# Attention and experts on one core: ScalarE copies the attention output out of PSUM, GpSimd divides it

## The reference

```python
x = x + xattn(layernorm(x), ctx)      # 16 heads of 32, 2048 keys
x = x + ffn(layernorm(x))             # 32 experts, the best 4 of a token, and a shared one
# in xattn, for each head:
q, k = fq_sym(q * scale), fq_sym(k)   # rounded to 8 bits per row
v = fq_sym(v, axis=keys)
attn = fq_unsigned(softmax(q @ k.T))  # rounded to 0..255 of the row's maximum
out = attn @ v
return concat(out) @ Wp + bp
```

## Time and profile before

| what | value |
|---|---|
| runs | 1444.52, 1453.22, 1441.58 us |
| median | 1444.52 us |
| profiled execution | 1447.9 us, of it a span of 1446.2 |
| mean granted TensorE clock | 0.978 |
| busy: TensorE / VectorE / ScalarE / GpSimd | 88 / 68 / 55 / 60 % of the span |

### The profile page before, as it was taken

One profiled execution on the slowest core, in us unless ns is written; L12 is line 12 of the kernel. 1 busy time (PEld: TensorE's weight loads), 2 busy tenths in 40 slices (PEclk: granted clock), 3 DMA queues, 4 the chain that ended last, 5 costly groups with the idle time before them and its releaser, 6 DMA issues.

```text
span 1446.2 us, 28685 instructions
## 1 busy us (share of the span) xinstructions
PE 1276.8 (88%) x7890; PEld 634.9 (44%) x7891; DVE 976.3 (68%) x1886; ACT 800.0 (55%) x1030; POOL 874.8 (60%) x894
## 2 busy tenths in 40 slices
PE   8999578888888888888887879999999999999995
PEld 3444134444444444444443434444444444444442
DVE  4567799999999999999999646823333333333332
ACT  2224499999999999999999742221222222222221
POOL 3223388899899999899888812243444444444443
PEclk9999799999999999999999889999999999999998
DMA  7565977786677667666677866465677777686442
GB/s 249 131 153 118 174 122 138 142 146 145 133 145 145 139 132 142 142 144 137 144 139 132 183 204 168 93 170 119 151 194 212 200 197 179 142 221 140 91 75 31
DMA packets 398568, 215.53 MB, mean 149 GB/s; under 512 B 356903, under 2 KB 357031, under 8 KB 398514
## 3 DMA queue, kind: packets, MB, share of 16 engines
q1 hardware_dynamic: 378338, 176.05, 51.7%
q0 software_dynamic: 20176, 38.83, 15.0%
HBM read 100.28 MB, written 37.49 MB: 95 GB/s over the span
## 4 chain that ended last, share of the span: by engine, by line
PE 36%; DVE 20%; issue 19%; DMA 13%; POOL 4%; ACT 4%; SPq 1%; DVEq 1%; POOLq 0%; ACTq 0%
PE psS L815 15%; DMA out_y<-mem 9%; DVE mem L579 7%; DVE mem L595 7%; PE psS L823 6%; PE psS L450 3%; POOL mem L669 3%; DMA mem<-mem 3%; ACT mem L536 2%; PE psS L1671 2%; PE psT L1280 1%; PE psP L807 1%; PE psAV L421 1%; DVE mem L1078 1%; PE psAV L1658 1%
## 5 line engine op out<-in xcount | busy, mean ns | idle before, releaser
L536 ACT ACTIVATE mem<-mem 128x2048 uint8<-128x2048 f32 x256 | 534.3, 2088 | 46.0 <-POOL mem L652 42.2
L669 POOL TENSOR_SCALAR mem<-mem 128x2048 bf16<-128x2048 uint8 x256 | 486.0, 1899 | 26.8 <-DMA mem<-mem 6.4
L450 PE MATMUL psS<-mem 128*128 128x512 bf16 x1024 | 313.2, 388 | 112.3 <-DVE mem L579 54.2
L815 PE MATMUL psS<-mem 128*128 (+1 forms) x752 | 348.6, 605 | 0.0
L595 DVE TENSOR_SCALAR_CACHE_REDUCE mem<-psS,mem 128x1024 f32<-128x1024 f32 x256 | 327.5, 1279 | 3.0 <-PE psS L450 2.9
L579 DVE TENSOR_SCALAR_CACHE_REDUCE mem<-psS 128x1024 f32<-128x1024 f32 x256 | 312.4, 1220 | 14.0 <-PE psS L450 11.8
L849 DVE TENSOR_SCALAR mem<-psS 128x512 f32<-128x512 f32 x94 | 64.9, 691 | 321.7 <-PE psS L815 312.5
L843 ACT ACTIVATE mem<-mem 128x256 f32<-128x256 f32 x94 | 39.1, 416 | 352.9 <-DVE mem L849 349.4
L1212 POOL DMA_INDIRECT out_y<-mem x78 | 124.3, 1593 | 170.4 <-DMA out_y<-mem 150.2
L815 PEld LDWEIGHTS psS<-mem 128*128 128x128 f32 x752 | 136.3, 191 | 146.7 <-issue 143.5
L823 PE MATMUL psS<-mem 128*128 (+1 forms) x376 | 179.0, 598 | 2.0 <-ACT mem L837 2.0
(11 more groups left out here) (210 smaller groups left out, 1177.1 us busy)
## 6 DMA issues: line engine op xcount, KB each, us to landing
mem<-in_moe_w SPq DMA_DIRECT2D x64, 768.0 KB, 5.7
mem<-xn_dram SPq DMA_DIRECT2D x32, 256.0 KB, 3.0
xn_dram<-mem SPq DMA_DIRECT2D x29, 256.0 KB, 2.2
mem<-in_x SPq DMA_DIRECT2D x28, 256.0 KB, 2.9
mem<-mem SPq DMA_TRANSPOSE x292, 3.1
mem<-in_ctx_in SPq DMA_DIRECT2D x16, 256.0 KB, 3.4
out_y<-mem SPq DMA_DIRECT2D x16, 256.0 KB, 2.2
mem<-in_wkv SPq DMA_DIRECT2D x2, 1024.0 KB, 7.8
```

What stands on the lines that cost most here:

```text
L450: last = nc.tensor.matmul(psS[c][:, k * D:(k + 1) * D], qT[pm][:, hm, :], kT[:, hm, c * HALF + k * D:c * HALF + (k + 1) * D], start=True, ...
L536: nc.scalar.activation(p8[slot], S[slot], ACT.Exp, bias=NB[:, slot:slot + 1], scale=sq[p][:, h:h + 1], accum_out=Z[p][:, h:h + 1]).then_in ...
L669: nc.gpsimd.tensor_scalar(pb[slot], pT[slot].bitcast(U8).rearrange("p (j q b) -> p j b q", b=2, q=P), 1.0, 0.0, ALU.mult, ALU.add).then_in ...
L815: last = nc.tensor.matmul(bankG[o], xT[o if xo is None else xo][:, c, :], w(c * 2 * I, 2 * I), start=(c == 0), stop=(c == DC - 1))
```

## The change

ScalarE copies the 128x512 outputs of a tile from `psAV` to a buffer in SBUF, `product_sb`, in step 7, ahead of that step's exponential. GpSimd multiplies this buffer by 1/Z into `an` at the end of its step 7, ahead of the scale of the queries (L628), and signals `attn_done`. VectorE keeps the reciprocal and loses the multiplication. The copy of the transposed output to `anT`, on ScalarE, moves from step 7 to step 8. TensorE's list isn't changed. `product_sb` lies in a part of SBUF that only the stage of the keys uses.

```diff
--- before.py
+++ after.py
@@ -136,6 +136,7 @@
         vT = cut(DC * TK).rearrange("p (c t) -> p c t", c=DC)
         vT8 = cut(DC * TK // 4, I8).rearrange("p (c t) -> p c t", c=DC)
         ks = [cut(D) for _ in range(2)]
+        product_at = at[0] - 2 * D
         behind_keys = at[0]
         k8 = cut(D // 4, I8)
         kr = cut(D)
@@ -153,6 +154,7 @@
         anT = cut(D).rearrange("p (c t) -> p c t", c=DC)
         x1 = cut(D)
         xn2 = cut(D)
+        product_sb = mem[:, product_at:product_at + D]
         at[0] = behind_keys
         p8 = [cut(TK // 4, U8) for _ in range(NS)]
         pT = [cut(TK // 4, U16) for _ in range(NS)]
@@ -226,6 +228,7 @@
 
 
         attn_done = sem("attn_done")
+        product_out = sem("product_out")
         attn_ev = sem("attn_ev")
         attn_mm = sem("attn_mm")
         attn_tr = sem("attn_tr")
@@ -514,7 +517,13 @@
             if h == 0 and there(t + 1):
                 act.wait_ge(query_tr, t + 2)
                 nc.scalar.activation(xnT.rearrange("p c t -> p (c t)"), psT[:], ACT.Copy).then_inc(query_ev, 1)
-            if h == 7 and there(t - 1):
+            if h == LAG and there(t - 1):
+                if due(H * t):
+                    act.wait_ge(av_done, H * t)
+                if due(t - 1):
+                    act.wait_ge(attn_done, t - 1)
+                nc.scalar.activation(product_sb, psAV[1 - p][:], ACT.Copy).then_inc(product_out, 1)
+            if h == 8 and there(t - 1):
                 if due(t):
                     act.wait_ge(attn_tr, t)
                 if due(t - 1):
@@ -581,12 +590,9 @@
             if h == LAG and there(t - 1):
                 if due(H * t):
                     dve.wait_ge(av_done, H * t)
+                if due(t - 1):
+                    dve.wait_ge(attn_done, t - 1)
                 nc.vector.reciprocal(rz, Z[1 - p]).then_inc(rz_ready, 1)
-                if due(t):
-                    dve.wait_ge(rz_ready, t)
-                if due(t - 1):
-                    dve.wait_ge(attn_tr, t - 1)
-                nc.vector.tensor_tensor(hv(an), hv(psAV[1 - p][:]), bc(rz, HD), ALU.mult).then_inc(attn_done, 1)
             if h == 8:
                 dve_scale(dve, t + 1)
             if within(n - 1):
@@ -674,6 +680,16 @@
                     pool.wait_ge(x1_ready, t)
                     apart(pool, t)
                 nc.gpsimd.tensor_scalar(minus_mean, x1_sum, -1.0 / D, 1.0, ALU.mult, ALU.mult).then_inc(mean_ready, 1)
+            if h == LAG and there(t - 1):
+                if due(t):
+                    pool.wait_ge(rz_ready, t)
+                    apart(pool, t)
+                    pool.wait_ge(product_out, t)
+                    apart(pool, t)
+                if due(t - 1):
+                    pool.wait_ge(attn_tr, t - 1)
+                    apart(pool, t - 1)
+                nc.gpsimd.tensor_tensor(hv(an), hv(product_sb), bc(rz, HD), ALU.mult).then_inc(attn_done, 1)
             if h == 2 and there(t - 2):
                 pool_root(pool, 1, t - 2)
             if h == 3 and there(t - 2):
```

## The result

The kernel with the change takes 1553.2 us (median of 4 runs, 1549.96 to 1556.51) where the kernel before takes 1445.5 on the same chip (4 runs): a ratio of 1.074, 95% interval 1.069 to 1.079, or 108 us more. The prediction was 1565, in a range from 1526 to 1588. The profiled execution of after took 1554.0 us around a span of 1552.2; the span of before was 1446.2, so 106 us are to be found between the two traces.

What follows compares the result with a forecast made beforehand. VectorE was taken to set the pace of the 41.0 us tile, GpSimd and ScalarE almost full. First tile 7, 14 rings 109 and last tile 5 made 121 us, on 1444.5 giving 1565; range 1526 to 1588.

Steps and rivals of the forecast that it cites:

- The mechanism: TensorE's transposes at step 8 wait for GpSimd's late step 7, idling about 7 us; forecast 1565 us, chance 0.64.
- The ring without the clock: Per tile, a loop of waits through GpSimd, TensorE and VectorE: 46.5 us where the tile was 41.0, at full clock.
- The load alone: TensorE doesn't stand and only GpSimd's added work counts: 0.7 us a tile, 11 us in all, 1455 us.
- The first tile: First multiplication under scores, t=1: VectorE's next head 4.6 us later, 6.9 with the lost clock.
- The 14 rings: Tiles t=2 to 15, each 48.8 us with the lost clock, 7.8 over the tile before: 109 us.
- I take 2.26, the row that shows the place: Extra time per tile for TensorE's start at low clock, read at t=15 of the kernel before: 2.26 us.
- The last tile: t=16, without scores: the multiplication stands behind the first indirect add, so the transposes come 4.9 us later.
- Rival 1: TensorE's wait is there but the clock isn't lost or is back at once: 34 us less, 1531 us; chance 0.16.
- Rival 2: The multiplication is early enough for TensorE and only GpSimd's load counts: 11 us, 1455 us; chance 0.06.
- Rival 3: VectorE is the only limit and loses its multiplication L589: 11 us faster, 1434 us; chance 0.03.
- Rival 4: Low clock costs 3.4 us each tile and the multiplication takes 1.9 us: 1593 us; chance 0.11.
- L522 ... costs after its move what it did: ScalarE's copy of the transposed output, moved from step 7 to step 8, was to add nothing.

Runs made afterwards that it cites:

- experiment 5: Changed kernel plus unread f32 128x512 products on TensorE ahead of its wait for the divided output: 1533.5 us with six, 1582.5 us with twelve.
- experiment 1: Kernel before, VectorE still dividing, plus one wait: TensorE's transposes also wait until GpSimd has scaled the queries in step 7: 1541.8 us, 1.067.
- experiment 4: Changed kernel with TensorE's transposes and the projection's first part at step 11, its other parts at steps 12 to 15, ScalarE's transposed copy at step 9: 1474.7 us.
- experiment 2: Kernel before plus an unread multiplication of the same size at the end of GpSimd's step 7: 1454.8 us, 1.0065.
- experiment 9: Kernel before with VectorE's multiplication L589 on one column in place of 512: tile of 40.67 us; total of 1468 us not comparable.
- experiments 7 and 8: Changed kernel with reciprocal, copy and multiplication at step 4: 1473.8 us; the same with x's second normalisation on ScalarE at step 3: 1449.9 us.
- experiments 1, 5 and 6: experiment 1 and experiment 5 as listed; the last: changed kernel plus an unread second GpSimd multiplication, directly ahead of the real one 1575.8 us, directly behind 1548.8 us.

## Why the prediction was right, and where its sizes were off

**The mechanism was right.** TensorE was to stand about 7 us in one piece: 7.01. The first multiplication was to start at 226.5: 226.4. The ring without the clock was to be 46.5: 46.3 to 46.4 in experiment 5. The load alone was to give 1455: 1454.8 (with VectorE's division still in it). What tells it from the rivals is experiment 1: one wait added to the kernel before makes 96 of the 108 us, and experiment 4: with the wait met in time they leave the tiles.

**The sum, term by term**, to the span's 106 where 121 stood:
- The first tile: 6.9 predicted. Head 10 starts at 232.98 where it was 227.18: 5.8.
- The 14 rings: 109 predicted. At t=15 head 10 starts at 902.14 where it was 802.80, 99.3 later, so the rings made 93.5. This is the term that was mis-sized. The step is "I take 2.26, the row that shows the place": the clock costs 1.4 a tile, 0.86 less, 12 us over 14. The row was of a stretch in which the clock came back later: before has 0.63 from 801 to 802 us, so it was back at about 801.7, 5.1 us after the transposes began at 796.63; in after it is back 3.3 us after they begin. The ring without it was 0.1 shorter, 1.4 us, as the multiplication took 1.05 us where 1.15 was taken. And the row's own tile was counted as if before had lost nothing there, though its head 10 stood 8.5 us behind the division (794.28 to 802.80), where at t=1 it was 7.3 (219.93 to 227.18): 1.3 us. Together these are 14.7 of the 15.7 by which the term was too large.
- From there to the last down projection, nothing predicted: the copy that ends it comes at 932.04, where by the prediction's 835.1 and these 99.3 it would be 934.4. 2.4 us were absorbed by slack at the end of the attention.
- The last tile: 4.9 predicted, 4.8 measured (transposes at 936.59, 101.7 behind the 834.90 of the earlier trace rows, and 96.9 were there already). The path is the one predicted, copy, indirect add, multiplication: from the add's start at 933.62 its 1.83 us and a multiplication of 1.05 would end at 936.50, and the multiplication ends at 936.53. Its record there is longer and overlaps that of the add (below).
- After the last transposes, nothing predicted: 4.3 us more. In the 64 us behind them the granted clock is 0.89 (938 to 1002) where it was 0.95 (836 to 900); that this is the cause wasn't tested.

5.8 + 93.5 - 2.4 + 4.8 + 4.3 = 106. That the two terms at which nothing was predicted, -2.4 and 4.3, nearly cancel is luck.

**Rival 1** (no clock lost, 1531) is about what experiment 5 gives with the clock held (1533), but in after the clock is lost in every tile looked at. **Rival 2** (load only, 1455) is experiment 2. **Rival 3** (VectorE's relief) is experiment 9: 5 us if all else could be had free, where 11 was its bound. **Rival 4** took the clock for 3.4 and the multiplication for 1.9; they are 1.4 and 1.05.

**A step that was right only behind a cover.** "L522 ... costs after its move what it did" held in after. In experiments 7 and 8 the same move is a wait of TensorE of up to 1.8 us, because then no ring hides it. The sentence named ScalarE's work behind the move and not who waits for the moved copy.

## What to carry to other kernels

Before work is moved to another engine, look up in the order of time where that engine's queue stands at the moment the consumer asks, not how busy it is. Here GpSimd was busy for 91% of a tile and could take the work at 9 us by load, but its step 7 ended 6 us after TensorE's step 8 began, and an in-order TensorE took scores, maxima and biases down with it: a wait that closes a ring through a lagging engine costs most of the lag, every turn (here 5.4 us a tile with the clock held, 6.8 without). An unread instruction put ahead of and behind the release tells such a ring from a loaded engine in two runs. And relief of the fullest engine is worth only what it is ahead of the next one (here 0.3 of 0.69 us).

## What the runs showed of the hardware

The tensor-tensor of 128x512 f32 on GpSimd, second input a broadcast one, takes 1.05 us, between the bounds of 0.77 and 1.53. At the last tile its record is 1.59 us long and begins 1.32 us into the record of an indirect add. Since it ends within 0.03 us of where the two one behind the other would end, this doesn't show that GpSimd worked on both at once; the two records only overlap:

```profile
933.62 1.83 POOL L1228 DMA_INDIRECT out_y<-mem,own_rows  x1 [3.19 <-ACT mem L947]
934.94 1.59 POOL L692 TENSOR_TENSOR mem<-mem 128x512 f32<-128x512 f32 x1
```

Giving an idle TensorE unread work of 5.3 us keeps the clock in most tiles and wins 20 us here; in three tiles the clock fell regardless, and 10.5 us of it, longer than the gap of 7, cost 29. What a lost clock costs isn't one number: it came back some 3.3 to 5.9 us after the release, and the second head was there 5.2 to 6.3 us after the release, where 3.7 is the time with the clock held (experiments 1, 5 and 6). Where in its tile the clock changes differs with the ring's length, which I had not expected, and by what rule stays open.
